# Attention values moved by transfers, context tiles turned beside value tiles, and one exponential for a pair of heads

## The reference

```python
def attention(query, ctx):                 # 16 heads of 16
    q, k, v = heads(query @ Wq.T + bq), heads(ctx @ Wk.T + bk), heads(ctx @ Wv.T + bv)
    attn = softmax(einsum('bhqd,bhkd->bhqk', q, k) * 0.25)
    return merge(einsum('bhqk,bhkd->bhqd', attn, v)) @ Wo.T + bo

def ffn(x):                                # 256 -> 704 -> 256, every linear in blockwise FP4
    h = silu(fp4_linear(x, w_gate)) * fp4_linear(x, w_up)
    return fp4_linear(h, w_down)           # fp4: scale = max|block of 16| / 6, then round to a grid

x = x + attention(layernorm(x), ctx)
x = x + ffn(layernorm(x))
```

## Time and profile before

| | |
|---|---|
| three runs | 1804.56, 1801.16, 1804.52 us; median 1804.52 |
| the profiled execution | 1801.16 us, its span 1799.4 us |
| PE busy, share of the span | 1687.2 us, 94% |
| DVE, ACT, POOL busy | 1398.6, 1155.4, 528.4 us (78%, 64%, 29%) |
| exponentials (L870) | 1630, 887.6 us, mean 599 ns |
| chain that ended last, by engine | PE 74%, DVE 15%, ACT 7%, issue 3%, DMA 1% |
| granted TensorE clock | mean 0.984 of full speed |

### The profile page before, as it was taken

How to read it: one execution, slowest core, us unless ns; L and a number is a source line. 1 busy time by engine, 2 the same in 40 slices (tenths; PEclk the granted TensorE clock), 3 DMA queues, 4 the chain that set the end, 5 groups by cost and what they waited for, 6 DMA issues and landing times.

```text
span 1799.4 us, 26659 instructions
## 1 busy us (share of the span) xinstructions
PE 1687.2 (94%) x9600; PEld 658.4 (37%) x9600; DVE 1398.6 (78%) x1969; ACT 1155.4 (64%) x2335; POOL 528.4 (29%) x409
## 2 busy tenths in 40 slices
PE   3799789999999999999999999999999999989978
PEld 2332124333343343433443333433334334423425
DVE  6777887888868887788878888688877887688538
ACT  2366567776667666776667766676667766666651
POOL 4316340442107320152204421073201622012213
PEclk8899999999999999999999999999999999999989
DMA  6643432142323322043221423243220422300000
GB/s 147 151 77 92 90 77 37 47 116 38 55 37 96 91 49 50 13 110 73 55 52 44 118 40 55 37 96 90 50 48 12 108 40 43 52 1 1 7 18 12
DMA packets 98031, 109.09 MB, mean 61 GB/s; under 512 B 18788, under 2 KB 83308, under 8 KB 97900
## 3 DMA queue, kind: packets, MB, share of 16 engines
q1 hardware_dynamic: 93344, 103.26, 27.1%
q10 hardware_dynamic: 4556, 4.13, 1.1%
HBM read 76.78 MB, written 30.16 MB: 59 GB/s over the span
## 4 chain that ended last, share of the span: by engine, by line
PE 74%; DVE 15%; ACT 7%; issue 3%; DMA 1%; ACTq 0%; POOL 0%; SPq 0%; DVEq 0%; POOLq 0%
PE pvb L714 19%; PE st L685 18%; PE mx L699 9%; PE misc L632 7%; DVE cmx L941 6%; PE misc L582 5%; ACT prob L870 4%; PE misc L589 4%; PE misc L644 2%; PE misc L652 2%; PE misc L521 1%; PE misc L640 1%; PE misc L611 1%; PE misc L570 1%; PE misc L559 1%
## 5 line engine op out<-in xcount | busy, mean ns | idle before, releaser
L870 ACT ACTIVATE prob<-st 128x512 f32<-128x512 f32 x1630 | 887.6, 599 | 419.9 <-PE st L685 418.2
L941 DVE TENSOR_REDUCE cmx<-mx 128x2 f32<-128x1024 f32 x768 | 905.3, 1219 | 215.4 <-PE mx L699 211.7
L685 PE MATMUL st<-qstack,kstack 112*128 112x512 bf16 x1630 | 520.6, 386 | 32.6 <-ACT prob L870 20.0
L714 PE MATMUL pvb<-prob,vv 128*17 128x512 f32 (+1 forms) x3328 | 440.7, 601 | 0.6 <-ACT prob L870 0.6
L685 PEld LDWEIGHTS st<-qstack,kstack 112*128 112x128 bf16 x1630 | 128.4, 98 | 554.9 <-issue 315.7
L699 PE MATMUL mx<-kstack,qstack 48*128 48x512 bf16 (+1 forms) x2048 | 253.3, 336 | 32.8 <-DMA qstack<-scr_q 16.3
L1202 POOL TENSOR_TENSOR cin<-cin 128x400 f32<-128x400 f32 (+1 forms) x60 | 55.3, 922 | 418.6 <-ACT cin L798 418.6
L1235 POOL TENSOR_TENSOR ht<-ht,rh 128x704 f32<-128x704 f32 x29 | 40.2, 1385 | 425.0 <-DVE rh L917 425.0
L632 PE MATMUL misc<-wguT,rowsT 128*128 128x352 f32 x456 | 154.9, 462 | 0.0
L699 PEld LDWEIGHTS mx<-kstack,qstack 48*128 48x128 bf16 x2048 | 58.0, 94 | 195.7 <-issue 147.2
L632 PEld LDWEIGHTS misc<-wguT,rowsT 128*128 128x128 f32 x456 | 87.1, 191 | 41.4 <-issue 1.0
(11 more groups left out here) (201 smaller groups left out, 1593.3 us busy)
## 6 DMA issues: line engine op xcount, KB each, us to landing
kstack<-scr_k SPq DMA_DIRECT2D x384, 100.1 KB, 4.3
scr_k<-cin SPq DMA_DIRECT2D x48, 300.0 KB, 3.2
qstack<-scr_q SPq DMA_DIRECT2D x372, 32.0 KB, 1.9
cin<-ctx_in SPq DMA_DIRECT2D x8, 1280.0 KB, 6.6
scr_q<-qp SPq DMA_DIRECT2D x15, 384.0 KB, 5.4
scr_k<-cin SPq DMA_DIRECT2D x16, 300.8 KB, 4.4
xn<-x SPq DMA_DIRECT2D x8, 512.0 KB, 3.9
x<-x SPq DMA_DIRECT2D x8, 512.0 KB, 3.8
```

Source lines behind the costliest of these rows:

```text
L685: mm(score_bank(it, n, pair, h)[0:KROWS[kt], :], kstack[:, hd, KOFF[kt]:KOFF[kt] + KROWS[kt]], qstack[:, hd, :], start=True, stop=True).th ...
L714: last = mm(pvb[32 * h:32 * h + D + 1, :], vv[0:w, kt, HG * g + h, :], prob[0:w, n % 2, h, :], start=(kt == 0), stop=(kt == NKT - 1))
L870: activate(prob[0:KROWS[kt], n % 2, 2 * pair + h, :], score_bank(it, n, pair, h)[0:KROWS[kt], :], ACT.Exp, scale=SCALE).then_inc(exp_done[ ...
L941: v.tensor_reduce(cmx[:, g % 2, h0:h0 + 2, at:at + 1], products, op=ALU.max, axis=AX.X).then_inc(max_free, 1)
```

## The change

Three things change, with the slots, orders and buffers that belong to them.

1. **One exponential for a pair.** `exps` waits for both scores of the pair and issues one ScalarE instruction over both banks of `st`. `exp_done` has one semaphore per pair. The first score of a pair waits for the whole exponential of the pair before.
2. **Context tiles beside value tiles.** A `v` job outside the prologue has a guest: one context tile is transposed into the right half of `misc` behind the value product, for a batch later, and evacuated behind it. The second-half jobs `ctxT` go. Only the prologue and the first four slots of the first iteration turn pairs of tiles (`ctx2`).
3. **Values by transfers.** `vv` holds per pair of heads value, ones and value columns (16 each), so that each head's matmul has 32 columns: 16 values and 16 times the denominator. `pvT`, `attT` and `group_divided` go. SP moves each head's 16 rows of sums and 16 rows of denominators from `pvs` to `att` and `sums` (eight transfers of 32 KB per group; in the tail half of them by ScalarE's queue). VectorE divides a tile of 128x512 twice per batch: `values` in step 37 (first half of the heads) and step 3 of the next iteration. `o` reads `att` directly.

The queries now stand before the keys (steps 9 to 15), and in GpSimd's order the rounding of the late rows stands before the split of key piece 4. `xnT` shares memory with `mt`, `bvl` with `rowsT`. GpSimd's bias addition also waits for a value tile of step 1.

The diff, cut to its core:

```diff
 SLOTS = {
-    0: ([("v", 8, "att")], [("ctxT", 0, "early")]),
-    1: ([("v", 9, "att")], [("pvT", 3, "late")]),
-    2: ([("v", 10, "att")], [("attT", 0, "late")]),
-    3: ([("v", 11, "att")], [("attT", 1, "late")]),
-    4: ([("v", 12, "att")], [("ctxT", 1, "early")]),
-    5: ([("o", 0, "late")], [("ctxT", 2, "early")]),
-    6: ([("o", 1, "late")], [("ctxT", 3, "early")]),
-    7: ([("ctxT", 4, "early")], [("ctxT", 5, "early")]),
-    8: ([("ctxT", 6, "early")], [("xnT", 0, "early")]),
-    9: ([("k", 0, "early")], [("xnT", 1, "early")]),
-    10: ([("k", 1, "early")], [("nm", 1, "att")]),
-    11: ([("k", 2, "early")], []),
-    12: ([("q", 0, "early")], []),
+    0: ([("v", 8, "att")], [("ctx2", 0, "once")]),
+    1: ([("v", 9, "att")], [("ctx2", 1, "once")]),
+    2: ([("v", 10, "att")], [("ctx2", 2, "once")]),
+    3: ([("v", 11, "att")], [("ctx2", 3, "once")]),
+    4: ([("v", 12, "att")], []),
+    5: ([("o", 0, "late")], []),
+    6: ([("o", 1, "late")], []),
+    7: ([("xnT", 0, "early")], []),
+    8: ([("xnT", 1, "early")], []),
+    9: ([("q", 0, "early")], [("nm", 1, "att")]),
+    10: ([("k", 0, "early")], []),
+    11: ([("k", 1, "early")], []),
+    12: ([("k", 2, "early")], []),
     13: ([("k", 3, "early")], []),
-    14: ([("k", 4, "early")], []),
-    15: ([("q", 1, "early")], []),
+    14: ([("q", 1, "early")], []),
+    15: ([("k", 4, "early")], []),
     16: ([("k", 5, "early")], []),
     17: ([("k", 6, "early")], []),
-    18: ([("pvT", 0, "att")], [("xqT", 0, "late")]),
-    19: ([("k", 7, "early")], [("xqT", 1, "late")]),
+    18: ([("xqT", 0, "late")], [("xqT", 1, "late")]),
+    19: ([("k", 7, "early")], []),
...
-    31: ([("gate", 5, "late")], [("pvT", 1, "att")]),
+    31: ([("gate", 5, "late")], []),
...
-    41: ([("down", 2, "late")], [("pvT", 2, "att")]),
+    41: ([("down", 2, "late")], []),
...
 DVE_EXTRA = {
-    1: [("late", "norm", 3)], 5: [("late", "stats", 0)], 6: [("late", "stats", 1)], 7: [("late", "mean", 0)], 8: [("late", "root", 0)],
+    3: [("late", "values", 1)], 5: [("late", "stats", 0)], 6: [("late", "stats", 1)], 7: [("late", "mean", 0)], 8: [("late", "root", 0)],
...
+    33: [("late", "hscale", 2)], 34: [("late", "hpower", 2)], 35: [("att", "nm", 3)], 37: [("att", "values", 0)], 39: [("late", "hscale", 3)], 40: [("late", "hpower", 3)],
...
 POOL_WORK = {
-    0: [("late", "bias", 0)], 10: [("early", "k", 0)], 11: [("early", "k", 1)], 12: [("early", "k", 2)], 13: [("early", "q", 0)],
-    14: [("early", "k", 3)], 15: [("early", "k", 4)], 16: [("early", "q", 1), ("late", "xround", 0)], 17: [("early", "k", 5)], 18: [("early", "k", 6)], 20: [("early", "k", 7)],
+    0: [("late", "bias", 0)], 10: [("early", "q", 0)], 11: [("early", "k", 0)], 12: [("early", "k", 1)], 13: [("early", "k", 2)],
+    14: [("early", "k", 3)], 15: [("early", "q", 1)], 16: [("late", "xround", 0), ("early", "k", 4)], 17: [("early", "k", 5)], 18: [("early", "k", 6)], 20: [("early", "k", 7)],
...
-        vv = sb("vv", [128, NKT, H, D + 1])
+        vv = sb("vv", [128, NKT, H // 2, 3 * D])
...
+            def values_in(it, g, part):
+
+                sp.wait_ge(pvs_done, it.count(part, NG, g + 1))
+                c, s = divmod(g, 2)
+                if g == 0:
+                    need(sp, full["o"], it.count(part, 2, 0))
+                if s == 0:
+                    need(sp, att_ready, it.count(part, NC2, c))
+                for h in range(HG):
+                    row = HALF * s + D * h
+                    values, weights = 2 * D * h + D * (h % 2), 2 * D * h + D * (1 - h % 2)
+                    sp.dma_start(att[row:row + D, c, :], pvs[values:values + D, :]).then_inc(values_row[g], 16)
+                    if it.kind != "tail":
+                        sp.dma_start(sums[row:row + D, :], pvs[weights:weights + D, :]).then_inc(values_row[g], 16)
...
+                def context_tile(job):
+                    _, j, part = job
...
+                    w, o = KROWS[j], job_bank(it, job)
+                    for h in range(NC2):
+                        last = turn(o[:, h * 128:h * 128 + w], ctx_rows[0:w, j, h * 128:(h + 1) * 128], ident[0:w, 0:w])
+                    last.then_inc(full["ctxT"], 1)
...
-                        if not wide or n == WIDE and pair == 0:
-                            need(pe, exp_done[2 * (1 - pair) + h], it.count("att", STEPS, n + pair))
-                        elif n > WIDE:
-                            pe.wait_ge(exp_done[2 * pair + h], it.count("att", STEPS, n))
+                        if h == 0 and (not wide or n == WIDE and pair == 0):
+                            need(pe, exp_done[1 - pair], it.count("att", STEPS, n + pair))
+                        elif h == 0 and n > WIDE:
+                            pe.wait_ge(exp_done[pair], it.count("att", STEPS, n))
...
-                    for h in range(2):
-                        act.wait_ge(st_full, it.count("att", HG * STEPS, HG * n + 2 * pair + h + 1))
-                        activate(prob[0:KROWS[kt], n % 2, 2 * pair + h, :], score_bank(it, n, pair, h)[0:KROWS[kt], :], ACT.Exp, scale=SCALE).then_inc(exp_done[2 * pair + h], 1)
+                    act.wait_ge(st_full, it.count("att", HG * STEPS, HG * n + 2 * pair + 2))
+                    activate(prob[0:KROWS[kt], n % 2, 2 * pair:2 * pair + 2, :], score_banks(it, n, pair)[0:KROWS[kt], :, :], ACT.Exp, scale=SCALE).then_inc(exp_done[pair], 1)
...
+                def values_divided(part, c):
+
+                    for g in (2 * c, 2 * c + 1):
+                        dve.wait_ge(values_row[g], it.count(part, 128, 128))
+                    v.reciprocal(sums[:, :], sums[:, :]).then_inc(rec_ready, 1)
+                    dve.wait_ge(rec_ready, it.count(part, NC2, c + 1))
+                    v.tensor_tensor(att[:, c, :], att[:, c, :], sums[:, :], ALU.mult).then_inc(att_ready, 1)
...
                     if what == "bias":
                         pool.wait_ge(s_x1, c(16, 16))
+                        if it.kind != "tail":
+
+                            pool.wait_ge(free["v"], it.count("att", NKT, 10))
```

More of the change, by code:

```diff
@@ L123 @@
 PRE_SLOTS = {
-    5: ([("ctxT", j, "early") for j in range(7)], []),
+    5: ([("ctx2", j, "early") for j in range(7)], []),
     8: ([("xnT", j, "early") for j in range(2)], []),
@@ L333, in job_count, with tiles_turned, guest @@
         def job_count(it, job):
-            return it.count(job[2], PER[job[0]], job[1] + 1)
+            kind, j, part = job
+            if kind == "ctx2":
+                return (PAIRS if part == "once" else 0) + j + 1
+            if part == "once":
+                return j + 1
+            if kind == "ctxT":
+                return tiles_turned(it, part, j + 1)
+            return it.count(part, PER[kind], j + 1)
+        def tiles_turned(it, part, k):
+            return (it.batch(part) - 2) * NKT + NKT - 8 + k
+        def guest(it, job):
+            if job[0] != "v" or it.kind == "pre":
+                return None
+            part = {"early": "next", "att": "early"}[job[2]]
+            return ("ctxT", job[1], part) if part in it.parts else None
         def job_bank(it, job):
+            if job[0] == "ctxT":
+                return misc[:, 2 * 128:]
             b = BANKS.bank(it.kind, job)
@@ L537, in shared @@
                         before = BANKS.last("loop", 0)
[L538 to L539 removed]
+                        assert before == BANKS.last("first", 0) and before[0] == "v" and before[2] == "early"
+                        pe.wait_ge(free["v"], it.count("att", NKT, before[1] + 1))
+                        if "early" in it.parts:
+                            pe.wait_ge(free["ctxT"], tiles_turned(it, "early", before[1] + 1))
                     elif it.kind == "tail":
@@ L849, in take @@
                         raw_in(j // 2 + 2)
+                    if guest(it, job):
+                        take(guest(it, job))
                 def first_queries():
@@ L1010, in extra @@
                         split_maxima(part, k)
-                    elif what == "norm":
-                        group_divided(part, k)
+                    elif what == "values":
+                        values_divided(part, k)
                     elif what == "stats":
@@ L1050, in extra @@
                     elif what == "xpower":
+                        if "early" in it.parts:
+                            dve.wait_ge(full["q"], it.count("early", 2, 2))
                         link(v.tensor_scalar(mt[:, :].bitcast(I32), xa[:, :].bitcast(I32), EXPONENT, None, ALU.bitwise_and), part)
@@ L1148, in weight_powers @@
                         dve.wait_ge(wq_done, p)
+                    else:
+                        dve.wait_ge(full["q"], it.count("early", 2, 2))
                     w_linked(v.tensor_scalar(m.bitcast(I32), w.bitcast(I32), EXPONENT, None, ALU.bitwise_and))
```

135 lines of the change are left out of this document (70 added, 65 removed).

## The result

| | before | after |
|---|---|---|
| median of four runs each | 1803.67 us | 1904.88 us (1903.97 to 1906.26) |
| ratio | | 1.0564 (1.0546 to 1.0582) |
| span of the profiled execution | 1799.4 us | 1902.4 us |
| mean granted clock | 0.984 | 0.966 |

Slower by 101 us; the forecast was slower by 80, and 1904.88 lies in its range, near the upper end. The page of the kernel after: busy times, the chain, two groups, the new transfers.

The account below looks back on a forecast made before the run. Two clocks were taken to bound a step: TensorE's queue and the scores-exponential-scores loop. Loop +9.6 six times, +58; first iteration +12, last +6, tail +4.5: in all +80 on the median, 1884 us, range 1838 to 1910.

Parts of the forecast that it names:

- The merged exponential: Each pair of scores: starts at 0.68, takes 1.03 us, second pair at 1.77; value and empty steps become 3.83 us.
- eleven late starts: Steps 18 to 37 of the loop: later starts add 1.3 us, against 1.4 less for transposes gone.
- The guest beside the value tile: Value steps: a context tile's two transposes, about 0.37 us, end at 1.68, under 1.77, and cost nothing.
- The rounding ahead of the split: Loop step 17: ScalarE waits for GpSimd's split of key piece 4, TensorE idles; +5.3 us an iteration.
- Rival A: Loop, step 17: rounding is early enough or nobody waits for the split of piece 4; 1842 us, chance 0.12.
- The clock behind it: Step after the split's stall: runs at a granted clock of 0.50; +1.7 us an iteration, ends 0 and 3.4.
- The division: VectorE, twice per batch: reciprocal 3.44 us, multiply 0.65; +2.5 us at step 38, +1.0 around steps 3 to 5.
- First iteration: First iteration: empty or weight steps 8, value steps 3, division 1; +12 us together.
- Tail: After the last copy, up to the output product: transfers 3.4 us and division 4.1; +4.5 us.
- Rival C: Idle stretches lower the clock more often, once more per iteration after the division, and the exponential costs 1.20; 1925 us, chance 0.11.
- Rival B: Every step: TensorE's own work is the bound, so six transposes gone save 28 us; 1776 us, faster, chance 0.07.

Follow-up runs that it names:

- e2: Changed kernel with two exponentials of 512 per pair and a semaphore per head, as before the change: 1839.16 us, 1.0201 of the kernel before.
- e5: Kernel before with the merged exponential alone, one instruction and one semaphore per pair: 1874.07 us, 1.0394 of the kernel before.
- e3: Changed kernel with two exponentials of 512 per pair, still waited for and released by pairs: 1933.07 us, 1.0726 of the kernel before.
- e1: Changed kernel with the split of key piece 4 before the rounding of the late rows again: 1868.67 us, 1.0369 of the kernel before.
- e8: Kernel before with the split of key piece 4 moved behind the rounding of the late rows: 1848.63 us, 1.0255 of the kernel before.
- e7: Changed kernel, merged exponential kept, with piece 4 split before rounding, late-row transposes in second halves of steps 18 and 19, division in halves: 1837.56 us, 1.0193.
- e4: Changed kernel with a copy of 16 columns in place of the reciprocal, transfers and multiply kept: 1875.63 us, 1.0406 of the kernel before.
- e6: e7 with two exponentials and a semaphore per head in place of the merged one: 1767.89 us, 0.9807 of the kernel before.

## Why the prediction was right, and where it was short

**The merged exponential**: right in mechanism and size. Forecast: length 1.03, start 0.68, second pair 1.77, maxima products 2.30, empty and value step 3.83. Measured: 1.02, 0.70, 1.78, 2.32 and 3.86. Key steps 4.04 to 4.10 (forecast 4.05), gate and up steps 3.86. For the eleven late starts in steps 18 to 37 the prediction has 1.3 us, though its own +0.15 each makes 1.65; in steps 20 to 37 without 31 they cost 1.9 together, and that is 0.6 of the 1.3 by which the stretch was missed. e2, e5 and e3 show that the cost is the pairwise start and release, as the prediction had it; the 0.06 that it lets one instruction save on a pair (1.03 for 1.09) came out as 0.06 a step in e3.

**The guest beside the value tile**: right that it costs nothing here. What the expectation of e2 has for single exponentials was wrong: maxima products at 2.21, measured 2.06. That is 0.15 for each of thirteen value steps, some 12 us over the six loop iterations of the 21 by which e2 came out under its expectation; 6.5 more lie in the first iteration, which gained 15.5 for the 9 expected.

**The rounding ahead of the split**: right, to the tenth. L1123's end 2.45 into step 16, measured 2.47; end of the split 6.95 into step 17, measured 7.05; step 17 9.35, measured 9.20 on average. e1 takes it away, e8 makes it anew. Rival A, that nobody waits for the split, is refuted by both.

**The clock behind it**: the term that was mis-sized. Forecast 1.7; step 18 was 4.47 before and is 6.86, 2.4 more, at a clock of 0.50 to 0.54 in all six loop iterations. Another cost hides behind it, which e1 shows. Without the stall that step is 5.46 at full clock, and 4.44 in e7, where the transposes of the late rows are back in the second halves: the change had moved them into the first half, ahead of the rows' being ready. I had followed the rounding only to the split behind it and not to its own reader. In the stall of after this wait is hidden, for L576 starts there without one, and the half clock acts on the whole step.

**The division**: right. Reciprocal 3.34 for 3.44; multiply 0.69 for 0.65 (half of a reduction of 2.35 / 2 is 0.59, so the forecast's own working gives less). Step 38 is 6.84 for 4.24 in e4, so it costs 2.6 there (forecast 2.5), and 0.8 in steps 0 to 9 (1.0). The 3.34 gives 6.5 ns per element, and from 512 to 256 elements, e6, it is (3343 - 1743) / 256 = 6.25 ns. What I drew from the Trainium skill (VectorE: DVE Perf Modes, First, the fixed hardware budget), a repeat count of 8 read as eight cycles, 4.3 us, is not what this chip does; the measurement decides.

**First iteration**: +17.1 for +12. Steps 0 to 17 grew by 3.2 and steps 26 to 38 by 1.6, as empty steps do. Steps 18 to 25 went from 36.2 to 40.7: 2.5 of that is in e1 as well, and 1.6 is a half clock in steps 18 and 19 (windows at 0.81 and 0.84, 9.8 us for 8.2 in e1). The order of GpSimd does not bring it: in this iteration there are no late rows to round, GpSimd's operations stand in the same order in after and e1, and TensorE's second scores of step 18 wait alike for the exponential, 1.45 and 1.46; with the order of after, e2 and e3 run both steps at 1.00. Why the clock fell in one and not in the other no run shows. Steps 39 to 51 went from 47.9 to 55.8: 3.6 goes with the division (e4), of which I had 1, since I left out the clock behind it; in e3, which has the same division, they took 54.1.

**Tail**: +6.4 for +4.5. Transfers from the end of the copy (1833.56) to the reciprocal (1837.79) took 4.2 for 3.4, division 4.07 as forecast, and the output product ran at the half clock after 7.95 us of idle, four matmuls in 2.07 for 1.13 just before.

The sum of what was short, in span: 12 in the loop (1.3 in the third stretch and 0.7 in the fourth, six times), 5 in the first iteration, 2 in the last, 1 in the start, 2 in the tail: 22 or 23 of 103. The start is no effect of the change that I can name: it lies between 78.1 and 79.4 in all ten executions, without an order. Rival C, more half clock and an exponential of 1.20, is right in its first half (first iteration, tail, sometimes behind step 38) and wrong in its second.

Rival B, that TensorE's work is the bound, is refuted for this kernel, but not foolish: with its two obstacles away (e6) the kernel is 34 us faster than before, and B had said 28 (for the value transposes alone, so that the nearness is in part chance). What I treated as one rival was really the value of the other parts, hidden behind the exponential.

What stays open: what brings the half clock in steps 18 and 19 of the first iteration, and a part of the 3.8 us that e6 still has over the kernel before in steps 39 to 51 there (51.8 for 47.9). 2.6 of them are in step 43, 6.74 for 4.15: VectorE runs a half reciprocal of 1.75 from 255.09 on, the reductions of two steps queue up behind it, and a maxima product waits for them, at full clock:

```profile
258.49 0.39 PE L764 MATMUL mx<-kstack,qstack 48*128 48x512 bf16 x2 [1.58 <-DVE cmx L1011]
```

No experiment varied either.

## What to carry to other kernels

When an instruction is merged with its neighbour, price its events before its time: where a double buffer hands work to and fro, a later start and a later release lengthen every turn (here 94 us), and the start-up saved (28 us at most) doesn't pay for it. When a piece of work is moved in an engine's order, follow both sides: who stands behind it now, and whether its own reader still comes late enough. Before a change is given up as slower, take its parts singly: here two of them together, freed of the third and of two waits, were worth 1.9%.

## What the runs showed of the hardware

- One exponential of 1024 elements over two banks took 1.02 us; two of 512 in a row 1.08, one of 512 alone 0.60. The second instruction overlaps the first, so merging saves 0.06.
- An idle TensorE can pay twice. After 5.26 us without a product the clock was 0.50 for the whole next step (7.06 us) and 1.00 in the one after. After the 7.95 us of the tail four matmuls at 0.50 took 2.07 for 1.13.
- Behind shorter waits the clock fell in some executions and not in others. In the first iteration step 39, with products in 3.01 of 5.10 us, was followed by one at 0.50; in e3, with products in 2.92 of 4.95, by one at 1.00. In e1 the wait of 1.75 in step 18 left the clock at 1.00 in five loop iterations and at 0.76 in one. In e3 two steps of the last iteration ran at 0.50 and 0.51, though the waits of TensorE in the steps ahead of them were of 1.24.
- The same VectorE operation (L1123, 128x1024) took 0.69 us in after, with GpSimd idle, 1.33 in e1 beside a split on GpSimd, and 1.53 before. Reordering one engine changed the durations on another.
- A transfer of 32 KB from `pvs` to `att`, both in the core's own memory, landed in 2.4 us in the median; those of the same size from HBM to `qstack` in 1.9.
